# A three-layer graph attention with its edge scores in feature-by-edge matrices, the gathered rows turned by an fp32 product with the identity

## The reference

```python
def _gatv2_layer(x, src, dst, edge_e, Wl, bl, Wr, br, att_w, bias):
    gl = (x @ Wl + bl).reshape(n, HEADS, CH)
    gr = (x @ Wr + br).reshape(n, HEADS, CH)
    xj = gl[src]
    e = xj + gr[dst] + edge_e
    e = jax.nn.leaky_relu(e, negative_slope=0.2)
    alpha = jnp.einsum('ehc,hc->eh', e, att_w)
    m = jax.ops.segment_max(alpha, dst, num_segments=n)
    alpha = jnp.exp(alpha - m[dst])
    denom = jax.ops.segment_sum(alpha, dst, num_segments=n)
    alpha = alpha / (denom[dst] + 1e-16)
    out = jax.ops.segment_sum(xj * alpha[..., None], dst, num_segments=n)
    return out.reshape(n, HEADS * CH) + bias
...
for i in range(N_LAYERS):          # three layers
    edge_e = (edge_attr @ We[i]).reshape(-1, HEADS, CH)
    h = _gatv2_layer(h, src, dst, edge_e, Wl[i], bl[i], Wr[i], br[i], att_w[i], bias[i])
    h = _batch_norm(h, gamma[i], beta[i])
    h = jax.nn.leaky_relu(h, negative_slope=0.02)
```

## Time and profile before

| | |
|---|---|
| median of 3 runs | 6846.17 us (6832.88 to 6849.38) |
| the profiled execution | 6835.19 us |
| its span | 6833.4 us, mean granted PE clock 0.908 |
| first gather of the attention layers | 3469.42, 4586.52 and 5705.38 us |
| PE, DVE, ACT, POOL busy | 5228.6, 4419.9, 2485.9, 4656.5 us |

### The profile page before, as it was taken

The page is one execution under the profiler, slowest core; times in us unless marked ns, Lnnn a source line. Parts: engine busy times, 40 slices in busy tenths (PEclk is TensorE's granted clock), DMA queues, the critical chain, the costliest instruction groups (busy, mean ns, idle before and its releaser), DMA issues.

```text
span 6833.4 us, 117887 instructions
## 1 busy us (share of the span) xinstructions
PE 5228.6 (77%) x33433; PEld 4525.5 (66%) x33433; DVE 4419.9 (65%) x15206; ACT 2485.9 (36%) x9471; POOL 4656.5 (68%) x4868
## 2 busy tenths in 40 slices
PE   8988851888888788788667777767777776777776
PEld 7555541777777677777556666656666665666675
DVE  5434330777676788877757777765766774777776
ACT  2554420777776587777501111110111111111112
POOL 1777776777776477777357777737777764777772
PEclk9999985999999899999879999978999997989887
DMA  2111111544444355544134444434444443444442
GB/s 65 41 39 39 42 24 57 131 126 126 126 126 112 94 151 151 147 142 142 52 108 136 140 135 132 138 79 129 136 140 133 131 121 93 136 135 135 132 132 68
DMA packets 496381, 755.03 MB, mean 110 GB/s; under 512 B 226141, under 2 KB 358593, under 8 KB 494709
## 3 DMA queue, kind: packets, MB, share of 16 engines
q1 hardware_dynamic: 314500, 425.53, 19.9%
q0 software_dynamic: 180928, 315.57, 19.4%
q10 hardware_dynamic: 320, 6.40, 0.4%
HBM read 647.92 MB, written 98.34 MB: 109 GB/s over the span
## 4 chain that ended last, share of the span: by engine, by line
POOL 20%; PE 15%; DVE 13%; issue 11%; DMA 4%; DVEq 2%; ACT 1%; POOLq 0%; ACTq 0%
POOL AR L577 13%; POOL AR L569 7%; PE PS L1342 5%; DVE AR L1938 4%; PE PS L1358 4%; PE PS L1355 3%; DMA AR<-gtab_d,AR 3%; DVE AR L2007 2%; DVE AR L2018 1%; DVEq L505 1%; DMA AR<-ptab_d,AR 1%; PE PS L1256 1%; PE PS L1232 1%; PE PS L1253 1%; DVE AR L2028 1%
## 5 line engine op out<-in xcount | busy, mean ns | idle before, releaser
L577 POOL DMA_INDIRECT AR<-gtab_d,AR x2436 | 2310.8, 949 | 848.2 <-issue 702.1
L569 POOL DMA_INDIRECT AR<-ptab_d,AR x1624 | 1546.7, 952 | 529.1 <-issue 476.7
L1358 PE MATMUL PS<-AR,ident 128*128 128x140 f32 x4872 | 1115.5, 313 | 246.2 <-DMA AR<-gtab_d,AR 243.0
L1342 PE MATMUL PS<-AR 128*112 128x132 f32 x4872 | 895.5, 318 | 395.8 <-DVE AR L1938 368.7
L1355 PE MATMUL PS<-AR 128*128 x4872 | 1093.5, 309 | 68.1 <-issue 67.9
L1342 PEld LDWEIGHTS PS<-AR 128*112 128x112 f32 x4872 | 704.3, 200 | 542.2 <-DVE AR L1938 259.0
L1358 PEld LDWEIGHTS PS<-AR,ident 128*128 128x128 f32 x4872 | 846.8, 212 | 311.2 <-DMA AR<-gtab_d,AR 309.5
L551 POOL DMA_INDIRECT rec_d<-AR x782 | 771.3, 986 | 371.0 <-issue 235.3
L1023 ACT ACTIVATE AR<-AR 128x448 f32<-128x448 bf16 x609 | 335.3, 570 | 1776.2 <-PE PS L1342 1598.5
L2018 DVE SCALAR_TENSOR_TENSOR AR<-PS,AR 128x280 f32<-128x280 f32 x1218 | 536.9, 445 | 674.9 <-PE PS L1358 672.6
L1256 PE MATMUL PS<-AR,ident 128*128 128x160 f32 x3248 | 790.3, 325 | 223.1 <-DMA AR<-ptab_d,AR 218.3
(11 more groups left out here) (347 smaller groups left out, 7417.4 us busy)
## 6 DMA issues: line engine op xcount, KB each, us to landing
AR<-ste_d SPq DMA_DIRECT2D x404, 512.0 KB
AR<-nbb_d SPq DMA_DIRECT2D x303, 224.0 KB
ste_d<-AR SPq DMA_DIRECT2D x101, 512.0 KB
AR<-gtab_d,AR POOLq DMA_INDIRECT x2436
AR<-ptab_d,AR POOLq DMA_INDIRECT x1624
nbb_d<-AR SPq DMA_DIRECT2D x101, 224.0 KB, 2.4
AR<-key_d SPq DMA_DIRECT2D x94, 224.0 KB
AR<-rec_d SPq DMA_DIRECT2D x812, 8.0 KB
```

Of the source, the lines that this page charges most:

```text
L569: e.indirect_dma_start(out=XJ1[:, t % 32, :], out_offset=None, in_=tabs_d[0][:, :], in_offset=off).then_inc(done_, 16)
L577: e.indirect_dma_start(out=xj2(t)[:, t % 4, :], out_offset=None, in_=tabs_d[1][:, :], in_offset=off).then_inc(done_, 16)
L1342: x = e.matmul(PS[6 + v_ % 2][0:B, (t % 2) * 132:(t % 2 + 1) * 132], SQ4[:, i % 4, t % 4, :], PX[:, i % 5, t % 4, :, :].rearrange("p h c - ...
L1358: x = e.matmul(o, ident[:, :], xj2(t)[:, t % 4, :], start=False, stop=True, skip_group_check=True)
```

## The change

The three layers' scores are computed with features on partitions and edges on columns. The 128 features are reordered on the host so that the four heads of one channel are neighbours (`by_head`), and gathered rows have 132 columns (128 and four ones) for 140.

- PE, `pair`: per tile, a product of the gathered rows (as weights) with the identity turns them, and a product of the block's rows of `TABG`, copied to a fixed place (`expander`), with `STE` is added. Four tiles fill one bank.
- ACT copies `TABG`'s block for each tile (new, `expander`), and then adds the bias of `gr` while it moves the bank to `LE` (new).
- DVE does the leaky relu on 512 columns in place (`leaked`) in place of `terms` and the sums.
- PE sums over features with a product of a shifted attention matrix `ATW` (new `scores`, one a tile), a round later than `pair`; it collects a chunk's scores already turned, so L1366 goes.
- The table of rounds weights one quad a round, chunks are 8 quads up to the 184th and then 6, 5, 4 and 4; there are 27 for 29, and LASTR is 217 for 214.
- Around the layers `gat_weights` is one operation instead of some thirty, ACT takes the rows of `TABG` out of the bank (`gat_out`), and the products alternate between two banks each instead of four.

```diff
-    ends = list(range(8, 153, 8)) + list(range(157, 198, 5)) + [NQ]
+    ends = list(range(8, 185, 8)) + [190, 195, 199, NQ]
...
-        for i in range(start, end):
-            r = max(back + 2 - gap, px[-1] if px else 0)
-            while px.count(r) >= 2:
-                r += 1
-            px.append(r)
+        back = max(turn + 3, px[-1] + 1 if px else 0)
+        px += [back + i for i in range(end - start)]
...
+                for j in range(-2, LASTR):
+                    if j + 2 < NQ:
+                        i = j + 2
+                        if i >= 3:
+                            w.wait_ge(s_e, pair_at(l, 2 * (i - 3) + 1))
+                        for t in range(4 * i, 4 * i + 4):
+                            x = e.activation(expander(t), TABG[:, bass.ds(block_of(cx, "scalar", t), 1), :].rearrange("p a f -> p (a f)"), ACT.Copy)
+                        done(x, s_ex)
...
+                    if 0 <= j < NQ:
+                        w.wait_ge(s_e, pair_at(l, 2 * j + 1))
+                        if j >= 2:
+                            w.wait_ge(s_lin, quad_at(l, j - 2))
+                        done(e.activation(LE[:, j % 2, :], PS[j % 2][:, :], ACT.Identity, bias=BRC[:, l % 2:l % 2 + 1]), s_le)
...
-                            o = PS[u % 4][:, (t % 2) * GW:(t % 2 + 1) * GW]
+                            o = PS[(u // 2) % 2][:, (t % 4) * 128:(t % 4 + 1) * 128]
+                            w.wait_ge(*gath_sem(l + 2, t))
+                            e.matmul(o, xj2(t)[:, t % 4, 0:128], ident[:, :], start=True, stop=False, skip_group_check=True)
                             w.wait_ge(*ste_sem(l + 2, t))
-                            e.matmul(o, STE[:, ste_slot(l + 2, t), (t % 8) * 128:(t % 8 + 1) * 128],
-                                     TABG[:, bass.ds(block_of(cp, "tensor", t), 1), :], start=True, stop=False, skip_group_check=True)
-                            w.wait_ge(*gath_sem(l + 2, t))
-                            x = e.matmul(o, ident[:, :], xj2(t)[:, t % 4, :], start=False, stop=True, skip_group_check=True)
+                            x = e.matmul(o, expander(t), STE[:, ste_slot(l + 2, t), (t % 8) * 128:(t % 8 + 1) * 128],
+                                         start=False, stop=True, skip_group_check=True)
...
+                        for kk in range(4):
+                            t = 4 * (i - chunk_start(c)) + kk
+                            x = e.matmul(PS[2 + c % 2][:, 0:128], ATW[:, 31 - t:159 - t], LE[:, i % 2, kk * 128:(kk + 1) * 128],
+                                         start=(t == 0), stop=(i == ENDS[c] - 1 and kk == 3), skip_group_check=True)
+                        done(x, s_lin)
...
+                def leaked(j):
+
+                    w.wait_ge(s_le, quad_at(l, j))
+                    done(e.scalar_tensor_tensor(LE[:, j % 2, :], LE[:, j % 2, :], 0.2, LE[:, j % 2, :], ALU.mult, ALU.max), s_att)
...
+                    add()
+                    if quads:
+                        weight(quads[0])
+                    add()
                     for n, step in ((0, scans), (1, carries), (2, args)):
...
-                        terms(2 * j)
-                        add()
-                        terms(2 * j + 1)
-                        add()
-                        scores(j)
-                        add()
...
+                        leaked(j)
                     while tiles:
                         add()
```

More of the change, by code:

```diff
@@ L182, in gnn_program @@
         BU = carve(161, 1)
[L183 to L186, removed]
+        ATT = gB[:, 0:1]
+        HEAD = gB[:, 4:8]
+        BRC = gB[:, 2:4]
+        ATW = nbeB[:, 0:159]
+        WLx = WPQ1[:, 0:128]
+        WEx = WPQ1[0:16, D:D + 128]
         ssq33, tw33, n33 = (carve(NB, B) for _ in range(3))
@@ L321, in gnn_program @@
         BL = BPQ[:, 0:128]
[L322 removed]
+        WRx = WU1[:, 0:128]
         den = Zf[:, NB * 128:NB * 132].rearrange("p (b h) -> p b h", h=4)
@@ L1005, in scalar_program, with gat_out @@
                     row_root(3)
+            def gat_out(l, b):
+                w.wait_ge(s_mm, mm_at(f"gat{l}", b))
+                done(e.activation(TABG[0:B, b, :], PS[6 + b % 2][0:B, 0:128], ACT.Copy), s_aev)
             for l in range(3):
@@ L1011, in scalar_program @@
                         done(e.activation(XT[:, g * TG:(g + 1) * TG], PS[g % 4][:, 0:TG], ACT.Copy), s_ts)
-                for j in range(LASTR):
+                if l == 0:
+                    for b in range(NB):
+                        gat_out(0, b)
+                w.wait_own()
+                w.wait_ge(s_tab, 128 + 80 * (l + 1))
+                cx = {}
+                for j in range(-2, LASTR):
[6 more added lines that the diff above has]
+                        done(x, s_ex)
+                    for i in weighted_in(j):
+                        w.wait_ge(*nl_sem(l, i))
+                        if i >= 4:
+                            w.wait_ge(s_scat2, pair_at(l, 2 * (i - 4) + 1))
+                        done(e.activation(SQ4[:, i % 4, :, :], NBB[:, nb_slot(l, i), :, :], ACT.Copy), s_oh2)
+                    if 0 <= j < NQ:
[3 more added lines that the diff above has]
+                        done(e.activation(LE[:, j % 2, :], PS[j % 2][:, :], ACT.Identity, bias=BRC[:, l % 2:l % 2 + 1]), s_le)
                     c = step_of(j, 3)
@@ L1018, in scalar_program @@
                         done(e.activation(FR, FD, ACT.Exp), s_f)
-                    for i in weighted_in(j):
-                        w.wait_ge(*nl_sem(l, i))
-                        if i >= 4:
-                            w.wait_ge(s_scat2, pair_at(l, 2 * (i - 4) + 1))
-                        done(e.activation(SQ4[:, i % 4, :, :], NBB[:, nb_slot(l, i), :, :], ACT.Copy), s_oh2)
                 p = ("gat1", "gat2", "fin")[l]
@@ L1045, in scalar_program @@
                 w.wait_ge(s_dve, DV[f"ab{l}"])
-                for g in range(7):
-                    done(e.activation(XT[:, g * TG:(g + 1) * TG], XT[:, g * TG:(g + 1) * TG], ACT.Identity,
-                                      scale=ST[:, 18:19], bias=ST[:, 19:20]), s_aff)
+                for g in range(9):
+                    if g < 7:
+                        done(e.activation(XT[:, g * TG:(g + 1) * TG], XT[:, g * TG:(g + 1) * TG], ACT.Identity,
+                                          scale=ST[:, 18:19], bias=ST[:, 19:20]), s_aff)
+                    if l < 2 and g >= 2:
+                        for b in range(4 * g - 8, 4 * g - 4):
+                            gat_out(l + 1, b)
             for g in range(8):
@@ L1402, in tensor_program @@
                         scat(v_)
+                    if 1 <= j <= NQ:
+                        scores(j - 1)
                 turn_groups(("gat1", "gat2", "fin")[l], H2, lambda g: DV[f"ov{l}_{g}"])
@@ L2155, in arrange @@
     h = lambda n: i["L1_gnn_" + n]
+    by_head = np.arange(128).reshape(4, 32).T.reshape(-1)
+    inner = lambda x: c(x[..., by_head])
+    layers = lambda x: c(np.stack([x[0], x[1][by_head], x[2][by_head]])[..., by_head])
     return {
```

185 lines of the change are left out of this document (72 added, 113 removed).

## The result

The changed kernel takes 6873.5 us (median of 5 runs, 6865.7 to 6887.6) against 6846.2 us (median of 5, 6832.9 to 6850.2). The medians differ by 27 us; the ratio worked out from all runs is 1.0051 with a 95% interval of 1.0034 to 1.0068: slower by about half a per cent. The forecast was 6849, with a range of 6795 to 6925. The profiled execution took 6878.7 us (span 6876.5), 43.5 us more than that of before.

The account below looks back on a forecast made before the run. POOL's gathers were taken to set the time. Profiled 6835.2 - 39 (tail) - 3 (around the layers) + 45 (longer gathers) = 6838; put on the median, 6846 + 3 = 6849 us, range 6795 to 6925.

Parts of the forecast that it names:

- What bounds the kernel: POOL's back-to-back gathers set the time in three stretches of 1015 us; savings on PE, DVE and ACT there are worth nothing.
- PE, ACT, DVE and the chain of a round: Per quad, PE's 3.9 us, ACT's 2.8 and a 4.7 us chain fit under POOL's 5.0; priced at nothing.
- Rival D: Chain of PE, ACT and DVE per quad exceeds POOL's 5.0 us, perhaps by lower clock; 6900 to 6990 us, chance 0.10.
- What lengthens a gather: In the gather stretches, `leaked` with two AR operands delays gathers that start during it: +45 us, bounds 0 and +71.
- when PE starves, a quad's last landing sets it: In the gather stretches, the last gather's landing fixes the phase of `leaked`: 4.0 to 4.7 us after its start, missing gathers.
- The round's own chain: From PE's last product through `LE`, `leaked`, additions and the next products: about 4.7 us at full clock, under POOL's 5.0.
- The random price: `leaked` meeting gathers at a random phase costs 0.12 us each on average, 71 us in all.
- rival C: In the gather stretches, `leaked` hits gathers at random or worse, costing 71 to 120 us: 6875 to 6924, chance 0.20.
- The tail: From a layer's last gather to its last addition: 51 us, 13 less a layer, 39 less in all.
- Rival E: After the last gather, additions remain one chain and the 39 us gain doesn't come: 6888 us, chance 0.06.
- Around the layers: One-operation `gat_weights` saves 3 us once before the first layer; table products and evictions between layers taken as 0.
- the forecast of no measurable change: Whole kernel's time stays within about 0.3% of before, 6826 to 6867 us; chance 0.39.

Follow-up runs that it names:

- the first lighter kernel: Changed kernel with node sums in one bank, not waited for and left out of the result, `leaked` done twice on AR operands: 8383.4 us, 0.9859 of the kernel before.

## Why the prediction was right, and where it was off

The time lies in the range and the mechanism was the one foretold, but by a term that was mis-sized: the lengthening of the gathers, put at 45 us, measured 74.

*What bounds the kernel.* POOL, as read: after the change too its gathers follow at their length plus 0.30, with 3.4 us of waiting for PE, and the stretches grew by what the gathers grew.

*PE, ACT, DVE and the chain of a round.* Right in what was drawn from it. PE's idle time behind additions is 290 us over all layers, and no stretch is longer for it. PE was busy for 857.25 / 203 = 4.2 us a quad, more than the 3.9 costed, and still had room in 5.1 (1044 / 203). Rival D asked for a round above 5.0; granted clock was 0.98 to 0.99 in the layers, where 0.88 and 0.91 had been, so the risk named for it did not come: PE had more to do (857 us busy in the first layer for 769) and its clock was higher.

*What lengthens a gather.* The mechanism was right, and this is the term that was mis-sized: 45 us forecast, 74 measured, just over the bound of 71. The timeline after, two rounds of one layer:

```profile
4104.84 0.95 POOL L576 DMA_INDIRECT AR<-gtab_d,AR  x1 [0.30 <-issue]
...
4104.87 0.69 DVE L2031 SCALAR_TENSOR_TENSOR AR<-AR 128x512 f32<-128x512 f32 x1 [1.97 <-ACT AR L1039]
...
4109.51 0.69 DVE L2031 SCALAR_TENSOR_TENSOR AR<-AR 128x512 f32<-128x512 f32 x1 [0.94 <-ACT AR L1039]
...
4109.83 1.19 POOL L576 DMA_INDIRECT AR<-gtab_d,AR  x1 [0.30 <-issue]
```

The first began 0.03 into a gather and cost nothing; the second was under way with 0.37 left and the gather took 0.24 more. In the whole trace 297 of 609 were under way at a gather's start, and those gathers are 67 us longer; where 0.2 us or more was left, the median is that rest less 0.127. The other 7 us lie with gathers that no `leaked` met; half of them (3.4) with the six that had begun 0.02 us ahead of one that followed another operation without a gap. The rule was read from few rows, and the third layer's were miscounted there: seven of its eight long operations lengthened a gather, by 3.3 us in all, not six.

The step that failed is "when PE starves, a quad's last landing sets it". I had `leaked` at 4.0 us behind the start of the quad's last gather; it came at a median of 5.5, a tenth before 4.7 and a tenth after 6.3. Only in a layer's first 20 rounds and its last few is the median below 5. PE's waits show why:

```profile
PE PS L1367 <- DVE AR L1954: 289.9, 361, 1.4
PE PS L1379 <- DMA AR<-gtab_d,AR: 243.6, 335, 6.7
```

It waited for additions (361 times) as often as for gathers. The round's own chain, estimated at 4.7 us, with a chunk's steps in it, would run close to POOL's 5.0 but not tied to it, so that the phase wanders; this is an argument and was not tested. 297 of 609 is 49%, and a random phase gives 0.69 / 1.25 = 55%. It isn't spread evenly: 153 of 609 began 0.25 to 0.35 us behind a gather's start, where they cost nothing and an even spread would put some 49. The random price (71) was still the one to take, and with it the forecast would have been 6849 - 45 + 71 = 6875. I had the argument for it in the text (rival C: so little room that the phase will wander) and gave it 0.20.

*The tail.* 51 us forecast, 50.9 to 51.8 measured; 39 forecast in all, 38.0 measured. The split is right in total, less so in its parts: the last sum follows the last gather by 5 us (7 said), and DVE then has 46 to 47 (44 said), since additions kept a pitch near the old one:

```profile
L1954 DVE TENSOR_TENSOR AR<-AR,PS 112x132 f32 x56 | 16.2, 289 | 17.8 <-PE PS L1367 13.0 <-DVE AR L1954 4.2 <-DVE AR L1949 0.7
L2023 DVE TENSOR_TENSOR AR<-AR,PS 128x528 f32<-128x528 f32 x12 | 8.4, 696 | 0.0
```

That is (16.2 + 17.8) / 56 = 0.61 us an addition, not 0.45; the clock was 0.65 there. These additions and weightings took 16.2 + 17.8 + 8.4 = 42 us, where I had 34, and the rest of the tail was shorter than I had it (4 for 10). So the agreement to a microsecond is luck in part. Rival E is out. That the smaller tail comes from the table of rounds is argued, not shown.

*Around the layers.* -3 forecast, -3.4 measured, hidden in the spans by 9.9 us of other origin further ahead.

*The sign.* The time lies in the range, and the forecast of no measurable change (0.39) did not come: at 1.0051 it is slower, to which I gave 0.35. Part of the nearness is luck: on the profiled executions the sum gave 6838 and 6878.7 came, 41 us more (29 from the gathers, 10 from ahead of the layers), but the profiled execution before lay 11 us below its median and the one after 5 above, so the medians miss by only 25.

## What to carry to other kernels

Where one engine issues gathers back to back and sets the time, look for DVE operations with both operands in on-chip memory: each that is under way when a gather begins adds its rest, less 0.13 us, to it. Price it with a random phase, (length - 0.13)^2 / 2 / pitch (77 us by the measured length of 0.692, where the changed kernel showed 74 in all). Where one event releases both engines the price can be nothing (543 of 609 in one harmless tenth of a microsecond) or nearly double (0.22 us a quad). Being hidden under another engine doesn't make such an operation free. Letting it read one operand from the accumulation bank took the lengthening away at the same length of operation; that this gives the 74 us back on a chip where POOL sets the time is argued from the equal sums, and was not measured.

## What the runs showed of the hardware

The hold goes one way, with two exceptions at its edge. In the changed kernel on the first chip the median length of the 446 `leaked` that began inside a running gather is 0.692, as of the others. But one that began just ahead of a gather was itself stretched, and the gather not:

```profile
4099.80 0.77 DVE L2031 SCALAR_TENSOR_TENSOR AR<-AR 128x512 f32<-128x512 f32 x1 [1.97 <-ACT AR L1039]
4099.85 0.94 POOL L576 DMA_INDIRECT AR<-gtab_d,AR  x1 [0.30 <-issue]
```

This holds for all 16 in this trace that began up to 0.045 us ahead of a gather after DVE's operation before had ended (0.72 to 0.77 us for 0.69), and for 313 in the first lighter kernel with both operands in AR; from 0.045 us on the gather is held for nearly the whole operation (1.46 us for 0.94). The other exception is the operation that follows another without a gap: it holds a gather that had begun up to 0.06 us before it (1.55 against 0.94 us, all 115 in the first lighter kernel). So a few hundredths of a microsecond decide between nothing and 0.6 us.

The Trainium skill, SBUF — State Buffer, in the section on the two separate sides, has whichever of a DVE operation with two SBUF inputs and a GpSimd operation that reads SBUF starts first hold the port pair for its whole instruction while the other fully blocks. The gather's side of it agrees (1.24 against 0.94 us), but for these edges, where the one that began first in the profile is the one held; that DVE would wait behind a running gather no run here shows.

And the same kernel, the one before, took 6846 us on the first chip and 8498 to 8572 on two others. In the changed kernel, traced on the first chip and on chip 2, operations have the same lengths and longer idle time between them (from PE's last product to ACT 0.31 and 1.68 us). The change is a loss of 0.5% on the first chip and a gain of 1.3% on chip 2. What makes the hand-overs longer is open.
